# Two of five row groups of product 1 as 2x2 blocks in seven products, with sums of blocks on GpSimd

## The reference, cut to what matters

```
h = relu(layernorm(x))
u = par_u[0]*par_u[1] * (diag_u[:,None]*h[:nu] @ W_u) + h[:nu]
i = par_i[0]*par_i[1] * (diag_i[:,None]*h[nu:] @ W_i) + h[nu:]
e = concatenate([u, i])
o = adj @ (adj.T @ e)            # product 1 is t = adj.T @ e, product 2 is adj @ t
out = x + layernorm(o)*gamma + beta + h
```

## Time and profile before

| what | value |
|---|---|
| median of three runs | 376.76 us |
| span of the profiled execution | 374.4 us |
| PE busy | 367.1 us (98%) |
| DVE busy | 251.5 us (67%) |
| ACT busy | 73.5 us (20%) |
| POOL busy | 23.7 us (6%) |
| DMA | 133.22 MB, mean 356 GB/s |

### The profile page before, as it was taken

One profiled execution on the slowest core, in us unless ns is written; L12 is line 12 of the kernel. 1 busy time (PEld: TensorE's weight loads), 2 busy tenths in 40 slices (PEclk: granted clock), 3 DMA queues, 4 the chain that ended last, 5 costly groups with the idle time before them and its releaser, 6 DMA issues.

```text
span 374.4 us, 8614 instructions
## 1 busy us (share of the span) xinstructions
PE 367.1 (98%) x3768; PEld 152.5 (41%) x3768; DVE 251.5 (67%) x249; ACT 73.5 (20%) x214; POOL 23.7 (6%) x30
## 2 busy tenths in 40 slices
PE   7999999999999999999999999999999999999995
PEld 5764455543334333433333343334333335436432
DVE  5999995859344965595289349754963793382366
ACT  4863012100032004000400320031004002202322
POOL 2023060000000000000000000000000000000036
PEclk9999999999999999999999999999999999999998
DMA  8999999999999999799969987997999699929603
GB/s 310 421 417 414 422 421 420 422 418 361 417 424 421 353 417 424 273 358 414 426 269 360 429 364 258 398 429 279 356 428 424 256 354 345 425 95 399 270 0 141
DMA packets 19896, 133.22 MB, mean 356 GB/s; under 512 B 2208, under 2 KB 2976, under 8 KB 4000
## 3 DMA queue, kind: packets, MB, share of 16 engines
q1 hardware_dynamic: 19440, 132.22, 87.4%
q10 hardware_dynamic: 432, 0.66, 0.5%
HBM read 131.55 MB, written 1.31 MB: 355 GB/s over the span
## 4 chain that ended last, share of the span: by engine, by line
PE 87%; DMA 7%; POOL 2%; SPq 2%; DVE 1%; issue 0%; ACT 0%; DVEq 0%; POOLq 0%
PE h_acc L756 35%; PE t_acc L782 32%; PE t_acc L725 10%; PE h_acc L739 9%; DMA natural<-adj_rows 7%; SPq L239 1%; POOL xs L360 1%; POOL scaled L356 1%; PE t_acc L800 1%; DVE xs L663 0%; SPq L236 0%; DVE scaled L652 0%; DVE natural L639 0%; PE h_acc L819 0%; DVE var L493 0%
## 5 line engine op out<-in xcount | busy, mean ns | idle before, releaser
L530 DVE STREAM_TRANSPOSE strips<-natural 128x2048 f32<-128x2048 f32 x76 | 168.2, 2274 | 48.4 <-PE h_acc L756 48.4
L756 PE MATMUL h_acc<-strips,centred 32*64 32x512 f32 x2432 | 133.3, 589 | 0.0
L782 PE MATMUL t_acc<-natural,e 128*64 128x512 f32 x560 | 121.4, 592 | 0.0
L756 PEld LDWEIGHTS h_acc<-strips,centred 32*64 32x64 f32 x2432 | 52.8, 132 | 78.5 <-issue 78.5
L782 PEld LDWEIGHTS t_acc<-natural,e 128*64 128x64 f32 x560 | 40.2, 137 | 79.9 <-issue 79.9
L725 PE MATMUL t_acc<-natural,e 128*64 128x256 f32 x480 | 54.1, 381 | 0.7 <-DMA natural<-adj_rows 0.6
L403 ACT COPY t_high<-t_acc 64x256 f32<-64x256 f32 x20 | 7.4, 368 | 212.6 <-PE t_acc L782 173.2
L539 DVE TENSOR_TENSOR t_sum<-t_acc,t_high 64x256 f32<-64x256 f32 x20 | 8.2, 410 | 57.0 <-ACT t_high L403 57.0
L725 PEld LDWEIGHTS t_acc<-natural,e 128*64 128x64 f32 x480 | 33.8, 137 | 20.6 <-issue 3.0
L410 ACT COPY centred<-centred 32x384 f32<-32x384 f32 (+2 forms) x60 | 24.2, 403 | 66.2 <-DVE centred L552 65.7
L739 PE MATMUL h_acc<-cols,centred 128*64 128x512 f32 x160 | 37.1, 599 | 0.0
(11 more groups left out here) (55 smaller groups left out, 86.6 us busy)
## 6 DMA issues: line engine op xcount, KB each, us to landing
natural<-adj_rows SPq DMA_DIRECT2D x100, 1024.0 KB, 11.8
cols<-adj_cols SPq DMA_DIRECT2D x20, 1024.0 KB, 7.6
natural<-adj_last SPq DMA_DIRECT2D x4, 1024.0 KB, 11.2
out<-xs SPq DMA_DIRECT2D x4, 256.0 KB, 2.0
xs<-x ACTq DMA_DIRECT2D x2, 256.0 KB, 5.4
xs<-x SPq DMA_DIRECT2D x2, 256.0 KB, 8.3
out<-xs SPq DMA_DIRECT2D x2, 128.0 KB, 2.0
smalls<-small SPq DMA_DIRECT2D x1, 150.0 KB, 3.3
```

The costliest lines, as they stand in the source:

```text
L530: nc.vector.transpose(strips[:, a, :, m].rearrange("p c t i -> p t c i"), natural[:, a, m].rearrange("p t (c j) -> p t c j", j=Q)).then_in ...
L756: last = nc.tensor.matmul(h_acc[D * s:D * (s + 1), q], t[part, a, b, u, :], rows, start=(isinstance(g, int) and g == 0 and b == 0 and u == 0),
L782: last = nc.tensor.matmul(t_acc[D * s:D * (s + 1), c].rearrange("p (a w) -> p a w", a=2), e[:, GT * m + 2 * k + s, :], natural[:, :, m, HA ...
```

## The change

In halves 3 to 8, row groups 4 and 3 (`SUMMED`) of product 1 are done in another way. For each k the two kinds of row tile (s) and the two panels (a) make a 2x2 matrix of blocks of `adj`, and the two kinds of tile and the two halves of the features (v) a 2x2 matrix of blocks of `e`. Plainly their product takes eight block products of 256 columns and 32 features; here it takes seven, of sums of blocks. GpSimd makes the four sums of `adj` for each group and pair (`add_blocks`), and once the sums of `e` (`forms`). The seven products times four k are laid out on four column quarters of the PE array (`LANES`), seven rounds. Results n = 2, 3, 4 and 1 are summed in PSUM in `t_acc` and in a new bank `x_acc`, and ACT and DVE combine them (`pair`, `keep_t_pair`).

Groups 0, 1, 2 of those halves, all of half 2 and product 2 from `cols` of panels 4 to 17 use the array as four column quarters of 32, as many moving columns as before. `t_acc` now has one bank for pairs, as the other PSUM bank went to `x_acc`; product 1 of a pair waits for both sums of the pair just before. `e` is centred once (`centre_e`), after panel 3's product 1, and DVE's reduction and subtraction for each panel after that are gone. Groups are taken in the order 0, 1, 4, 2, 3, turned in the order 0, 1, 3, 2, with the last two turns of a pair's second panel behind the work on t. A turn of the loop is one pair: strips, rest of the next pair (4, 2, 3), cols, first two groups of the pair after.

The diff, cut to its core:

```diff
+ORDER = (0, 1, 4, 2, 3)
+TURNS = (0, 1, 3, 2)
+BEHIND = 2
+SUMMED = (4, 3)
+LANES = (((1, 0), (1, 1), (1, 2), (1, 3), (2, 0), (2, 1), (2, 2)),
+         ((5, 0), (5, 1), (5, 2), (5, 3), (3, 0), (6, 2), (6, 3)),
+         ((6, 0), (6, 1), (4, 0), (4, 1), (4, 2), (4, 3), (2, 3)),
+         ((7, 0), (7, 1), (7, 2), (7, 3), (3, 1), (3, 2), (3, 3)))
...
+            for g in range(PAIRED + 2, LAST - 1, 2):
+                for a in range(2):
                     for m in range(EARLY):
+                        refill(g + a, m)
+                for m in (4, 3, 2):
                     for a in range(2):
+                        refill(g + a, m)
+                for a in range(2):
+                    refill_cols(g - 2 + a)
+            for m in TURNS:
+                refill(LAST - 1, m)
...
+            def add_blocks(half):
+                for m in SUMMED:
+                    for a in range(2):
+                        pool.wait_ge(s_natural[a][m], 16 * (half + 1))
+                    pool.wait_ge(s_first, firsts_pair(half - 1, m))
+                    nc.gpsimd.tensor_tensor(sum_of(m, 0), block_of(1, m, 0), block_of(1, m, 1),
+                                            ALU.add).then_inc(s_sums, 1)
...
-            def pair(g, half, c):
+            def pair(half):
+                act.wait_ge(s_first, firsts_pair(half, ORDER[-1]))
+                act.wait_ge(s_t_part, 2 * half)
+                nc.scalar.copy(t_high[:, 0:WIDE], t_acc[D:2 * D, 0, 0:WIDE]).then_inc(s_t_high, 1)
+                nc.scalar.copy(sixth, x_acc[2 * Q:3 * Q, 0:WIDE]).then_inc(s_sixth, 1)
+                nc.scalar.copy(other, first_v).then_inc(s_other, 1)
+                nc.scalar.copy(t_high[:, WIDE:2 * WIDE], t_acc[D:2 * D, 0, WIDE:2 * WIDE]).then_inc(s_t_high, 1)
...
+            for a in range(2):
+                keep_t_high(PAIRED + a, t_place(a), firsts_pair(FIRST_HALF, ORDER[-1]))
+                spread_t(PAIRED + a, a)
             pairs(act, pair)
...
+            def centre_e(m):
+                nth = ORDER.index(m)
+                dve.wait_ge(s_first, firsts(PAIRED - 1, m))
+                nc.vector.tensor_reduce(total[:, nth % 2], e[:, rows_of(m), :], AX.X, ALU.add).then_inc(s_e_total, 1)
+                dve.wait_ge(s_e_total, nth + 1)
+                nc.vector.scalar_tensor_tensor(e[:, rows_of(m), :], by_tile(total[:, nth % 2]), -1.0 / D,
+                                               e[:, rows_of(m), :], ALU.mult, ALU.add).then_inc(s_e_centred, 1)
...
+            def first_plain(half, m):
+                ready(half, m)
+                if m == ORDER[0]:
+                    pe.wait_ge(s_t_sum, 2 * half)
+                if isinstance(half, int) and half == FIRST_HALF:
+                    pe.wait_ge(s_e_centred, ORDER.index(m) + 1)
+                for k in range(HALF):
+                    for s, v in itertools.product(range(2), range(D // Q)):
+                        lane = slice(D * s + Q * v, D * s + Q * (v + 1))
...
+            def first_summed(half, m):
+                ready(half, m)
+                pe.wait_ge(s_sums, sums_done(half, m))
+                for i in range(len(LANES[0])):
+                    for lane in range(QUADRANTS):
+                        n, k = LANES[lane][i]
+                        weights_in, columns_in = product(m, n, k)
...
+            for m in ORDER:
+                first_plain(FIRST_HALF, m)
             second_loaded(PAIRED - 1, 1, PAIRED // 2 - 1)
-            first_pair(PAIRED // 2, 0, range(GROUPS))
+            first_early(FIRST_HALF + 1)
+            pe.wait_ge(s_forms, 4 * len(SUMMED))
+            with pe.Fori(FIRST_HALF, LAST_HALF - 1) as half:
+                strips_pair(half)
+                first_rest(half + 1)
+                loaded_pair(half)
+                first_early(half + 2)
+            strips_pair(LAST_HALF - 1)
+            first_rest(LAST_HALF)
+            loaded_pair(LAST_HALF - 1)
             for m in range(2 * EARLY):
                 first(LAST - 1, 0, LAST // 2, m)
-            second_pair(LAST - 3, LAST // 2 - 1)
+            strips_pair(LAST_HALF)
             for m in range(2 * EARLY, GROUPS):
                 first(LAST - 1, 0, LAST // 2, m)
+            loaded_pair(LAST_HALF)
```

More of the change, by code:

```diff
@@ L147, in pairs @@
         def pairs(eng, pair):
[L148 to L151, removed]
+            with eng.Fori(FIRST_HALF + 1, LAST_HALF + 1) as half:
+                pair(half)
         def firsts(g, m):
@@ L400, in keep_t_high @@
                 act.wait_ge(s_first, done)
-                if not (isinstance(g, int) and g == 0):
+                if g > 0:
                     act.wait_ge(s_t_sum, g)
-                nc.scalar.copy(t_high[:], t_acc[D:2 * D, bank, columns]).then_inc(s_t_high, 1)
+                if g == LAST - 1:
+                    act.wait_ge(s_t_part, g)
+                nc.scalar.copy(t_high[:, 0:WIDE], t_acc[D:2 * D, bank, columns]).then_inc(s_t_high, 1)
             def spread_t(g, a):
@@ L535, in keep_t, with turn_t @@
                 dve.wait_ge(s_t_high, g + 1)
-                if not (isinstance(g, int) and g == 0):
+                if g > 0:
                     dve.wait_ge(s_t_part, g)
                 bank, columns = place
-                nc.vector.tensor_tensor(t_sum[:], t_acc[0:D, bank, columns], t_high[:], ALU.add).then_inc(s_t_sum, 1)
+                nc.vector.tensor_tensor(t_sum[:, 0:WIDE], t_acc[0:D, bank, columns], t_high[:, 0:WIDE],
+                                        ALU.add).then_inc(s_t_sum, 1)
                 dve.wait_ge(s_t_sum, g + 1)
+                turn_t(g, a, slice(0, WIDE))
+            def turn_t(g, a, columns):
                 if not (isinstance(g, int) and g < PAIRED):
@@ L621, in _ @@
                 step(g, g % 2, g // 2)
-            pairs(dve, pair)
+            for m in ORDER:
+                centre_e(m)
+            turn_pair(FIRST_HALF, keep_t_plain)
+            pairs(dve, lambda half: turn_pair(half, keep_t_pair))
             for m in range(TURNED):
@@ L768, in step @@
                 second_strips(g - 1, 1 - a).then_inc(s_strips_done, 1)
[L770 to L786, removed]
@@ new lines, in place_of @@
+            def place_of(lane, n):
+                part = slice(Q * lane, Q * (lane + 1))
+                if n in (2, 3, 4):
+                    return t_acc[part, 0, WIDE * (n == 4):WIDE * (1 + (n == 4))]
+                rest = n == 6 and lane == 1
+                return x_acc[part, WIDE * rest:WIDE * (1 + rest)]
+            def first_summed(half, m):
[5 more added lines that the diff above has]
+                        weights_in, columns_in = product(m, n, k)
+                        last = nc.tensor.matmul(place_of(lane, n), weights_in, columns_in,
+                                                start=(m == SUMMED[0] and i == 0), stop=False, skip_group_check=True)
+                last.then_inc(s_first, 2)
@@ new lines, in first_rest, with first_early, loaded_quarters @@
+            def first_rest(half):
+                first_summed(half, 4)
+                first_plain(half, 2)
+                first_summed(half, 3)
+            def first_early(half):
+                for m in range(EARLY):
+                    first_plain(half, m)
+            def loaded_quarters(g, a, half):
+                pe.wait_ge(s_cols[a], 16 * (half + 1))
+                pe.wait_ge(s_t, g + 1)
+                for b in range(BLOCKS):
+                    for s, v in itertools.product(range(2), range(D // Q)):
+                        lane = slice(D * s + Q * v, D * s + Q * (v + 1))
+                        last = nc.tensor.matmul(h_acc[lane, LOADED], t[:, a, b, 0, Q * v:Q * (v + 1)],
+                                                cols[:, a, s, b], start=False, stop=False, skip_group_check=True)
+                last.then_inc(s_loaded_done, 1)
@@ L791, in second_pair, with strips_pair, loaded_pair @@
+            def strips_pair(half):
                 for a in range(2):
-                    second_loaded(g + a, a, half)
+                    second_strips(2 * half + a, a).then_inc(s_strips_done, 1)
+            def loaded_pair(half):
+                for a in range(2):
+                    loaded_quarters(2 * half + a, a, half)
             def last_columns(m, blocks):
```

205 lines of the change are left out of this document (152 added, 53 removed).

## The result

The changed kernel takes 379.6 us (median of four runs, 379.43 to 380.3) against 376.66 (376.23 to 376.93) in the same measurement: ratio 1.0079, interval 1.0058 to 1.01. It is 0.8% slower. The forecast was 376.5, its range ended at 378.8.

The account below looks back on a forecast made before the run. PE alone was taken to bind the kernel from 44 us on. Terms of -4.79 + 0.24 + 3.8 + 0.45 = -0.3 us against the median 376.76 gave 376.5 us; range 375.3 to 378.8.

Parts of the forecast that it names:

- its first rival: PE's clock falls in the wait before half 3: about 1.95 us lost, 378.4 us in all, chance 0.20.
- the new wait: Before half 3's product 1, PE idles some 3.1 us until both sums of half 2 are done.
- The end: Behind the last pair: three more changes of tile form and panel 18's late-requested group 2, +0.45 us (0 to 0.9).
- The range from the bounds: The forecast's own range around 376.5 us, stated as 375.5 to 377.6.
- the sum of -0.3: All terms together, in us: -4.79 + 0.24 + 3.8 + 0.45 = -0.3.
- the pairs: Six pairs: 12 summed groups save 4.79 us; the plain groups and cols on four tiles cost +0.24.
- The summed group: One group by seven products, 14 rounds of 216.8 ns: 3.035 us, 0.399 less than a plain group's 3.434.
- Half 2: First pair: PE waits for both sums of half 2 before half 3's product 1, +3.8 us (2.8 to 4.3).
- the second sum's chain of 4.89 us: Half 2: the second panel's sum ends 4.89 us after product 1, 6.31 before less 1.42 for reduction and subtraction.
- The wait of 0.5 for a load near 93: Half 2: PE waits for group 4's second panel, the opening backlog's last load, from 92.90 to 93.5 us.
- The four covers of the steady pairs: Second sum, DVE, GpSimd additions (2.5 us each) and DMA all keep up with PE in a pair, each put at 0.
- 1 ns a round: Cost of four tiles over two in each round; over 240 plain and cols rounds +0.24 us (0 to 1.4).

Follow-up runs that it names:

- plain_groups: The changed kernel with the seven products undone, groups 4 and 3 as plain groups on four tiles: 383.82 us, ratio 1.0184.
- warm_gap: The changed kernel with 12 matmuls of 256 columns that nothing needs put before half 3's waiting product 1: 377.78 us, ratio 1.0045.
- two_banks: The changed kernel with half 2 summing product 1 in t_acc's other bank, so half 3 waits only for panels 2 and 3: 373.39 us, ratio 0.9926.
- warm_half: The changed kernel with 6 filler matmuls, half of warm_gap's, before half 3's product 1: 378.63 us, ratio 1.005.
- both_orders: two_banks with panel 18's group 2 asked for before group 3 and half 2's groups in order 0, 1, 2, 4, 3: 372.4 us, ratio 0.9896.
- after_again: The changed kernel once more, unedited: 379.2 us, ratio 1.0071.

## Why the prediction was wrong

**The step that failed is the choice between the forecast and its first rival: whether PE's clock falls in the new wait.** The forecast took the wait of 3.1 us as costing 3.1 us, and put the fall of the clock at 0.20, because PE's work is dense on both sides. Density did not help: in all three profiles of the changed kernel, and that of plain_groups, the granted clock over 2 us behind the wait was 0.61 or lower, and with PE kept at work (warm_gap) it was 1.00. The Trainium skill ("TensorE: Matmul & The Clock Gate", Why this matters for your kernels) says that gaps in PE's work bring the lower level back. The profiles agree, with the 0.56 and the 8.77 us above. The price was right: 1.95 us forecast, 8.77 - 6.87 = 1.9 measured, 1.7 against warm_gap's 7.08. The prediction also read its own row too coarsely. It had the mean of 0.69 from 371.0 us on the earlier trace rows; the same trace, cut finer, has 0.50 from 372.5, which is 2.1 us behind PE's last work at 370.40 and so less than the 3.1 us that the forecast left it idle. That row gave the rival a larger chance than 0.20, though no certainty: at the end of the changed kernel the clock held for 2.8 us (1.00 up to 377.0, PE's last work ends at 374.23).

**The fall alone gives 378.4, which lies inside the range; the opening and the end carried the time out of it.** The prediction has no term for the opening, so it stood at nothing. In the profiled execution it is 1.95 us. The page's row for the loads of x on SP (us from issue to landing, the last figure) and PE's wait for the sums of x, first in the changed kernel (its wait of 1.8 us stands above), then in two_banks:

```profile
xs<-x SPq DMA_DIRECT2D x2, 256.0 KB, 9.5
...
xs<-x SPq DMA_DIRECT2D x2, 256.0 KB, 8.6
PE h_acc L858 <- DVE sums L580: 0.9, 2, 0.7
```

In the four profiles with a late opening (three of the changed kernel, warm_half) these loads took 9.5 to 10.2 us (the median of two), PE's longest wait for the sums of x was 1.8 to 2.4 us, and the clock fell behind it. In the eight others they took 7.6 to 9.0 us, no such wait was above 0.9, and the clock stayed. That is a pattern, not an experiment, and why x came late stays open: the code is the same up to there in all edits of the changed kernel, the DMA setting is excluded, and what the DMA engines moved does not separate the two (275 to 387 GB/s between 6 and 8 us in the late ones, 331 and 333 in plain_groups and both_orders, which were on time).

**The term "The end", +0.45, was too small.** Measured: +0.9 for panel 18's first groups, 0.6 of it the wait for group 2 behind group 3, and +0.3 behind them, where the tile form changes twice more. In the seven other profiles with the same order at the end PE waited there for 0.3 to 2.0 us.

**The range from the bounds was narrower than its own bounds.** The terms' lower and upper bounds add up to 374.4 and 379.4 against the median before, not to 375.5 and 377.6. The measured 379.6 lies above both, as neither sum has the clock or the opening in it. In the profiled execution the difference from the sum of -0.3 is made of +1.9 for the clock, +1.95 for the opening, +0.8 for the end, -0.3 for half 2 and -0.2 for the pairs.

**What held.** The summed group: 3.035 us forecast, 3.02 measured; the pair 33.9 and 33.89; the pairs -4.55 net and -4.7. Half 2: +3.8 forecast, +3.5 measured, with the wait of 3.1 us for `t_sum` to the tenth and the second sum's chain of 4.89 us at 4.90 (105.49 to 110.39). The wait of 0.5 for a load near 93 is not there in the changed kernel, where half 2 began 2 us later than forecast. The four covers of the steady pairs: no PE wait in the window of the pair, though an addition on GpSimd took 2.38 us, as this group by form has it, close to the 2.5 taken:

```profile
L413 POOL TENSOR_TENSOR sums<-natural 128x1024 f32<-128x1024 f32 x12 | 28.6, 2382 | 104.4 <-DMA natural<-adj_rows 89.9 <-PE t_acc L942 14.5
...
L979 PEld LDWEIGHTS x_acc<-sums,forms 128*32 128x32 f32 x240 | 16.1, 110 | 0.0
```

The weight loads, 110 ns each and four to a round of some 216 ns, cost nothing: the summed groups took 3.02 us without a gap. The Trainium skill (the same page, Part 3, The mechanism) says that a load overlaps running matmuls only where the row groups differ. By that rule, an estimate, the summed groups would have been some 1.5 us longer each (14 loads of 110 ns), and they are not.

For a clock that stays, the forecast was still low. warm_gap, with no fall in its profile and mean clocks of 0.996 to 0.999 in all six executions, has the wait in full and takes 377.78 us, 1.3 above the forecast; the end, with PE waiting 1.6 us, is the larger part of that. The two executions of the changed kernel at 376.6 and 377.7 were not profiled, so that the first lies at the forecast may be luck.

## What to carry to other kernels

A saving that is spread over many turns (0.39 us, twelve times) is undone by one new wait, so when a change gives up a buffer, look first at what its releases are queued behind: one copy moved ahead of six others, and the addition behind it ahead of the turns, took 379.2 us (after_again) to 373.35 here, part of which is the opening. Price a new wait of PE twice, as its length and as its length with the slow matmuls behind it (1.7 to 1.9 us here), and read the chance of the second from every row where PE was idle, the opening and the end too. Before trying to shorten it, fill it with matmuls that nothing needs, which shows the two apart. And let a queue ask for loads in the order in which they are wanted.

## What was not expected of the hardware

PE's clock fell behind single waits of 3.1 us with dense work on both sides (in all four profiles that have one), behind one of 2.0 us at the end of plain_groups, and behind those of 1.8 to 2.4 us in four openings. It stayed behind waits of 0.5 and 1.8 us at half 3 (warm_gap, warm_half) and of 1.6 to 1.9 us at the end (warm_gap, warm_half, after_again). So the length of the wait alone did not decide, and what else did is not shown. The low level lasted some 4 us each time, but some 6 in warm_half's opening. Four 128x32 fp32 tiles side by side need 3.43 us for 32 matmuls of 512 columns, 429 ns a round, as two 128x64 tiles do: two tiles more cost nothing that shows, where the forecast had put 1 ns a round.
